# Cross attention of a two-layer perceiver: another order of VectorE's work in a head's step, and the wide running maximum folded by two maxima

## The reference, cut to what matters

```
q = (layernorm(x) @ Wq).reshape(256, 16 heads, 128) / sqrt(128)
k = (ctx @ Wk).reshape(4096, 16 heads, 128)
v = (ctx @ Wv).reshape(4096, 16 heads, 128)
scores = q @ k^T per head             # 16 x 256 x 4096
attn = softmax(scores, over the 4096)
x = x + (attn @ v).reshape(256, 2048) @ Wo
```

## Time and profile before

| | |
|---|---|
| median of 3 runs | 1687.32 us |
| profiled execution, its own time | 1687.09 us |
| its span | 1685.1 us |
| TensorE busy | 1607.2 us, 95% |
| VectorE busy | 1185.3 us, 70% |
| ScalarE busy | 720.1 us, 43% |
| GpSimd busy | 192.7 us, 11% |
| granted TensorE clock | 9 or more tenths of full speed in each of 40 slices, mean 0.997 |

### The profile page before, as it was taken

One profiled execution on the slowest core, in us unless ns is written; L12 is line 12 of the kernel. 1 busy time (PEld: TensorE's weight loads), 2 busy tenths in 40 slices (PEclk: granted clock), 3 DMA queues, 4 the chain that ended last, 5 costly groups with the idle time before them and its releaser, 6 DMA issues.

```text
span 1685.1 us, 23090 instructions
## 1 busy us (share of the span) xinstructions
PE 1607.2 (95%) x8798; PEld 1251.7 (74%) x8798; DVE 1185.3 (70%) x2124; ACT 720.1 (43%) x981; POOL 192.7 (11%) x247
## 2 busy tenths in 40 slices
PE   9999999999899999999999999989899999999998
PEld 8887878888787888877887888777766857555454
DVE  5546787888778788878878888989674682633333
ACT  4434454445444445444444545545441361322221
POOL 0001101011100101010010101111100054021110
PEclk9999999999999999999999999999999999999999
DMA  7876545454555545464444444333511335579994
GB/s 231 235 221 192 158 119 145 131 157 117 174 140 138 144 132 153 110 179 116 134 132 113 135 118 126 94 100 99 196 76 50 122 129 217 249 212 409 423 424 180
DMA packets 125660, 283.48 MB, mean 168 GB/s; under 512 B 7728, under 2 KB 83696, under 8 KB 119408
## 3 DMA queue, kind: packets, MB, share of 16 engines
q1 hardware_dynamic: 103248, 201.27, 35.8%
q0 software_dynamic: 22304, 80.75, 16.7%
HBM read 207.51 MB, written 74.48 MB: 167 GB/s over the span
## 4 chain that ended last, share of the span: by engine, by line
PE 44%; DVE 24%; issue 23%; ACT 5%; DMA 3%; POOL 2%; SPq 0%; DVEq 0%; POOLq 0%; ACTq 0%
PE bank L41 11%; PE bank L502 6%; PE bank L2320 5%; DVE esum L944 4%; DVE mx L879 4%; PE bank L470 4%; DVE e_parts L955 3%; DVE S L923 3%; ACT S L693 2%; DVE k_lo L863 2%; PE bank L526 2%; PE bank L2359 2%; PE bank L1886 2%; PE bank L2345 2%; DVE v_out L960 1%
## 5 line engine op out<-in xcount | busy, mean ns | idle before, releaser
L502 PE MATMUL bank<-wv_parts,cT_hi 128*128 128x512 f32 x1024 | 333.7, 389 | 0.4 <-DMA wv_parts<-wv_dram 0.4
L693 ACT ACTIVATE S<-S 128x1024 f32<-128x1024 f32 (+1 forms) x129 | 135.9, 1053 | 226.7 <-DVE S L923 226.5
L502 PEld LDWEIGHTS bank<-wv_parts,cT_hi 128*128 128x128 f32 x1024 | 192.3, 188 | 40.7 <-DMA wv_parts<-wv_dram 0.8
L944 DVE TENSOR_TENSOR esum<-esum,S 128x256 f32<-128x256 f32 x360 | 152.9, 425 | 77.1 <-ACT S L693 67.5
L470 PE MATMUL bank<-cT_hi,wk_hi 128*128 128x512 f32 x512 | 201.0, 392 | 0.2 <-DVE cT_lo L856 0.2
L470 PE MATMUL bank<-cT_lo,wk_hi 128*128 128x512 f32 x512 | 199.7, 390 | 0.0
L470 PE MATMUL bank<-cT_hi,wk_lo 128*128 128x512 f32 x512 | 199.5, 390 | 0.0
L502 PE MATMUL bank<-wv_parts,cT_lo 128*128 128x512 f32 x512 | 199.4, 389 | 0.0
L41 PE MATMUL bank<-q_hi,k_hi 128*128 128x256 f32 x512 | 149.2, 291 | 42.1 <-DVE k_lo L863 42.1
L879 DVE TENSOR_TENSOR mx<-mx,S 128x256 f32<-128x256 f32 x390 | 165.3, 424 | 24.2 <-ACT S L687 14.0
L702 ACT CAST e_parts<-S 128x1024 fp32r<-128x1024 f32 (+1 forms) x129 | 135.0, 1046 | 96.9 <-PE bank L526 89.7
(11 more groups left out here) (327 smaller groups left out, 2797.5 us busy)
## 6 DMA issues: line engine op xcount, KB each, us to landing
w<-in_w_moe SPq DMA_DIRECT2D x32, 2304.0 KB, 15.7
v_dram<-v_out SPq DMA_DIRECT2D x112, 512.0 KB, 4.8
v_back<-v_dram POOLq DMA_DIRECT2D x110, 512.0 KB, 4.2
ctx_nat<-in_ctx SPq DMA_DIRECT2D x8, 1024.0 KB, 5.4
ctx_raw<-in_ctxT SPq DMA_DIRECT2D x7, 1024.0 KB, 8.8
v_dram<-v_back SPq DMA_DIRECT2D x14, 512.0 KB, 4.8
v_late<-v_dram POOLq DMA_DIRECT2D x14, 512.0 KB, 3.7
wv_parts<-wv_dram POOLq DMA_DIRECT2D x6, 1024.0 KB, 8.3
```

The costliest lines, as they stand in the source:

```text
L502: t = e.matmul(banks[b][:], l, r, start=(c == 0 and m == 0), stop=(c == DT - 1 and m == 2))
L693: e.activation(Sj, Sj, ACT.Exp).then_inc(raised, 1)
L944: t = e.tensor_tensor(total, l, r, ALU.add)
```

## The change

VectorE's order in heads 0 to 11 is written anew. In a step from 2 on it becomes split_e, split_k and shift (in steps 2 and 6 shift first), keep_max, split_v, and then the sum of this same chunk; before, the sum of the next chunk stood ahead of split_v. In step 0 split_e stands ahead of split_v and sum_e, and ScalarE's order follows (raise and round of chunk 0 ahead of round_v). The reciprocal of `scale_o` becomes a function of its own, in step 2, and its product moves to step 3; the splits of Wo and of o move to step 4. In heads 12 to 14 split_k of chunk 0 moves ahead of fold_sum and of the first shift, and split_k of chunk 7 behind keep_max and split_e. GpSimd's `add_sums(h - 1)` stands in step 1 of head h for all heads, behind that step's load of values. The reduction of the wide maximum becomes two maxima, 128x512 and 128x256.

```diff
--- before.py
+++ after.py
@@ -749,11 +749,11 @@
                         if h:
                             store_scores(h, NCH - 1)
                         round_k(h + 1, 0)
-                        for u in units(h, 0):
-                            round_v(u)
                         if h:
                             raise_scores(h, 0)
                             round_e(h, 0)
+                        for u in units(h, 0):
+                            round_v(u)
                         raise_scores(h, 1)
                         continue
                     if j == 1:
@@ -897,16 +897,21 @@
                     own.wait(e)
                     own.done(e.tensor_tensor(mx_late[:], mx_late[:], Sj, ALU.max))
                 if j == NCH - 1:
-                    own.wait(e)
                     e.wait_ge(max_ready, h)
                     e.wait_ge(y_projected, h - 1)
-                    e.tensor_reduce(mx_folded[:], mx_late[:].rearrange("p a t -> p t a"), AX.X, ALU.max).then_inc(max_folded, 1)
+                    fold_max().then_inc(max_folded, 1)
+
+            def fold_max():
+
+                own.wait(e)
+                own.done(e.tensor_tensor(mx_late[:, 0:2], mx_late[:, 0:2], mx_late[:, 2:4], ALU.max))
+                own.wait(e)
+                return e.tensor_tensor(mx_folded[:], mx_late[:, 0], mx_late[:, 1], ALU.max)
 
             def keep_last_max():
 
-                own.wait(e)
                 e.wait_ge(max_ready, XH - 1)
-                own.done(e.tensor_reduce(mx_folded[:], mx_late[:].rearrange("p a t -> p t a"), AX.X, ALU.max))
+                own.done(fold_max())
                 own.wait(e)
                 e.wait_ge(scored, NH)
                 own.done(e.tensor_reduce(mx_late[:, 0, :], twin[:].rearrange("p (a t) -> p t a", t=T), AX.X, ALU.max))
@@ -972,9 +977,11 @@
                 to = esum_t if h == SUMMED else mx
                 e.tensor_tensor(to[:], esum_late[:, 0], esum_late[:, 1], ALU.add).then_inc(sum_folded, 1)
 
-            def scale_o(h):
+            def invert_row(h):
                 e.wait_ge(sum_ready, h + 1)
                 own.done(e.reciprocal(esum_t[:], esum_t[:]))
+
+            def scale_o(h):
                 own.wait(e)
                 e.wait_ge(o_moved, h + 1)
                 e.tensor_tensor(oT[:], oT[:], esum_t[:], ALU.mult).then_inc(scaled, 1)
@@ -1037,60 +1044,62 @@
                 if piece_at(j, 1) is not None:
                     split_piece(piece_at(j, 1))
             for h in range(LATE):
-                for j in range(NCH):
-                    if j == 0:
-                        split_q(h + 1)
-                        if h:
-                            keep_max(h, NCH - 1)
-                            move_o(h - 1)
-                        split_k(h + 1, 0)
-                        if h:
-                            shift(h, 0)
-                        for u in units(h, 0):
-                            split_v(u)
-                        shift(h, 1)
-                        sum_e(h, 0)
-                        if h:
-                            split_e(h, 0)
-                        continue
-                    if j == 1:
-                        sum_e(h, 1)
-                        split_k(h + 1, 1)
-                        shift(h, 2)
+                split_q(h + 1)
+                if h:
+                    keep_max(h, NCH - 1)
+                    move_o(h - 1)
+                split_k(h + 1, 0)
+                if h:
+                    shift(h, 0)
+                shift(h, 1)
+                if h:
+                    split_e(h, 0)
+                for u in units(h, 0):
+                    split_v(u)
+                sum_e(h, 0)
+                split_k(h + 1, 1)
+                shift(h, 2)
+                split_e(h, 1)
+                keep_max(h + 1, 0)
+                for u in units(h, 1):
+                    split_v(u)
+                sum_e(h, 1)
+                if half_at(h, 1) is not None:
+                    split_half(half_at(h, 1))
+                for j in range(2, NCH):
                     split_e(h, j)
-                    keep_max(h + 1, j - 1)
-                    if j > 1:
+                    if j == 4 and h:
+                        split_qo("wo", h - 1)
+                        split_o(h - 1)
+                    if j in (3, 4, 5):
                         split_k(h + 1, j)
+                        shift(h, j + 1)
+                    else:
                         if j + 1 < NCH:
                             shift(h, j + 1)
+                        split_k(h + 1, j)
                     if j == NCH - 1:
                         split_wk(h + 2)
-                    if j == 1:
-                        for u in units(h, j):
-                            split_v(u)
-                        sum_e(h, 2)
-                    else:
-                        if j + 1 < NCH:
-                            sum_e(h, j + 1)
-                        for u in units(h, j):
-                            split_v(u)
+                    keep_max(h + 1, j - 1)
+                    for u in units(h, j):
+                        split_v(u)
+                    if j == 3 and h:
+                        scale_o(h - 1)
+                    sum_e(h, j)
                     if half_at(h, j) is not None:
                         split_half(half_at(h, j))
                     if j == 2 and h:
-                        scale_o(h - 1)
-                    if j == 3 and h:
-                        split_qo("wo", h - 1)
-                        split_o(h - 1)
+                        invert_row(h - 1)
                     if j == NCH - 2:
                         split_qo("wq", h + 2)
             for h in range(LATE, XH - 1):
                 split_q(h + 1)
                 keep_max(h, NCH - 1)
                 move_o(h - 1)
+                split_k(h + 1, 0)
                 if h > LATE:
                     fold_sum(h - 1)
                 shift(h, 0)
-                split_k(h + 1, 0)
                 shift(h, 1)
                 split_e(h, 0)
                 sum_e(h, 0)
@@ -1103,14 +1112,15 @@
                         shift(h, j + 2)
                     if j + 1 < NCH:
                         sum_e(h, j + 1)
-                    if j in (1, NCH - 2):
+                    if j == 1:
                         split_k(h + 1, j + 1)
                     keep_max(h + 1, j - 1)
                     if j + 1 < NCH:
                         split_e(h, j + 1)
-                        if j not in (1, NCH - 2):
+                        if j > 1:
                             split_k(h + 1, j + 1)
                     if j == 2:
+                        invert_row(h - 1)
                         scale_o(h - 1)
                     if j == 3 and h == LATE:
                         split_qo("wo", h - 1)
@@ -1217,9 +1227,7 @@
                         load_v(n + 3)
                     if h and j == 0 and n != TAIL:
                         largest_score(h)
-                    if j == NCH - 1 and h < LATE:
-                        add_sums(h)
-                    if j == 0 and LATE < h < XH - 1:
+                    if j == 1 and 0 < h < XH - 1:
                         add_sums(h - 1)
 
         CROSS_DONE = TT * 3
```

## The result

The changed kernel takes 1700.49 us, the median of 4 runs (1698.52 to 1700.57), against 1687.51 us for the kernel before (4 runs, 1687.03 to 1690.25): a ratio of 1.0071, 95% interval 1.0053 to 1.0088. The profiled execution took 1698.52 us. Forecast were 1684.0 us and a range of 1672 to 1693.

A forecast was written before the change was run, and what follows sets the result against it. TensorE was taken as the bound, with VectorE's order setting its stalls. From 1687.09 us, 12.6 won in early heads and 9.3 lost in heads 12 to 14 gave 1683.8, plus 0.2 for the median: 1684.0 us, range 1672 to 1693.

The forecast's parts named there:

- What bounds the kernel: Whole kernel: TensorE is the bound and VectorE's order sets its stalls, 48 us for ten early heads.
- the steady step: Early heads, new order: k_lo comes 1.2 us early, so S(3), S(4), S(7) wait no more.
- The wait that comes: Step 1 of each head: VectorE stands still 4.4 us for GpSimd's sum, S(1) is late; 3.0 us lost a head.
- Heads 4 and 8: No V in step 0: S(2) 4.6 us late, W(h,1) 0.2, S(0) keeps 1.6, W(h,0) 0.4; 6.8 each.
- Heads 12 to 14: VectorE has nearly no slack, so losses come out at S(4): 4.9, 2.6 and 1.8 us, 9.3 lost together.
- The fold: Late heads: the wide maximum's reduction takes 1.1 us for 2.01; the last fold, on the path, saves 0.8.
- The shift beside GpSimd's sum: Late heads: the shift took 2.12 us beside GpSimd's sum, against 1.21; in the new order it stands alone.
- the bound of 1640: Lower bound if the wait for the sum costs nothing: -3.0 x 9, and some 11 in the late heads.
- (a): Early heads' step 2: VectorE loses 0.9 at the first shift and S(2) stalls too; 1692 us, slower, chance 0.24.
- (d): Early heads' waits stay, as ScalarE's k_hi was their cause; only the losses count, 1723 us; chance 0.03.
- (b): Heads 12 to 14 find slack again and lose only what S(1) shows, 4.7 us; 1679 us; chance 0.17.
- (c): The wait for the sum hardly binds; all but S(0)'s waits go, 1640 to 1665 us; chance 0.08.

The follow-up runs named there:

- the filled kernel: The changed kernel plus identity matmuls on TensorE, 11 ahead of S(1) in heads 1 to 11, 16 ahead of S(2) in heads 4 and 8: 1686.21 us.
- the seventh experiment: The changed kernel with add_sums in step 0, plus 9 identity matmuls ahead of W(h,0) in heads 12 to 14: 1641.78 us, against 1639.94 without them.
- the eighth experiment: The changed kernel with add_sums in step 0, plus one reduction of the wide maximum in place of the two maxima: 1645.73 us, against 1639.94.

## Why the prediction was wrong, point by point

- **What bounds the kernel, and the steady step:** right. The waits at S(3), S(4), S(7) and W(h,0) of the early heads are gone, apart from the 0.2 at W(4,0) and W(8,0) (forecast 0.4).
- **The wait that comes:** right in place, chain and price. VectorE stands still 4.49 us for 4.4, the sum takes 1.75 for 1.74, the gap at S(1) is 2.6. A head where the clock stays up takes 72.41 us, W(6,0) to W(7,0), for 72.3.
- **Heads 4 and 8:** right in place; the gap at S(2) is 5.4 where 4.6 were given.
- **The term that failed is the price of that wait:** "With 0.1 for a restart the new loss is 3.0 us in each head". It was taken as idle time alone. The prediction traded 44 waits of at most 1.7 us for 14 of up to 5.4 with nearly the same sum, and left out that TensorE comes back from the long ones at half clock. In the ten heads that is 11.2 us: 734.7 to 745.9 between the filled kernel and the changed one. With it the ten heads come to -10.4 + 11.2 = +0.8; the rest of the measured +3.9, 3.1 us, is S(2)'s 0.8 in two heads, 0.1 of the period in the other eight, and some 0.7 that isn't accounted for. The span missed the forecast by 14.7 us: these 11.2 and 3.1, and 0.4 ahead of W(1,0). The clock turned the sign of the ten heads: with the wait kept and the clock held up they are 7.2 us faster than before.
- **Heads 12 to 14:** 9.3 us lost, forecast 9.3, and in part that is luck. Head 12 goes as forecast: k_lo(4) comes 25.9 us behind W(12,0) for 21.6, which with the late W(12,0) is the 5.4 of the prediction. But up to the columns' sums of head 14 the heads have lost 10.8 us (1.0 by the late W(12,0), then 161.7 us for 151.9), and 1.4 came back behind them: there TensorE is at half clock in both kernels, for 6.8 us before and for 3.4 us after, and needs 6.6 and 5.2 us to W(15,0). One link was missed, S(2) waits 1.8 us for ScalarE's store; VectorE sets the pace to S(4) all the same. That the half clock in the heads themselves (mean 0.96 up to the columns' sums) cost nothing is argued from the seventh experiment, which tested it at W(h,0) only.
- **The fold:** it takes 1.1 us for 2.0, as forecast, but by the eighth experiment it is worth 1.6 us in the three heads and not 2.7.
- **The shift beside GpSimd's sum:** in the changed kernel no shift takes over 1.22 us, so it does stand alone, as the prediction said; with the sum in step 0 it takes 2.12 again in heads 13 and 14.
- **Two slips in the working**, which change little above: the bound of 1640 comes to 1646 by its own terms (1684 - 27 - 11), and head 13 to 2.8 and not 2.6 (3.3 less a wait of 0.5).
- **Rivals:** none named the clock. (a) put its loss at S(2) of the early heads; S(2) of heads 1 to 3 waits for nothing. (d), also on the slower side, kept the early waits, and they went. (b) had heads 12 to 14 lose only half of what they lost, and (c) came true only when the sum was moved.
- **The range** reached 1693 by rival (a) and ended 7.5 us short. Its bounds were all for idle time. The kernel before had two signs to ask with. It fills waits elsewhere with matmuls that compute nothing (`stay_awake`, six of them ahead of W(15,0)). And its trace has a row: the clock fell to 0.5 at 1181.5, in its one wait of 3.9 us (the columns' sums wait for esum_t), as this row of a stretch of the kernel before shows:

```profile
1181.54:1188.37 6.83, 6.37 (x18) 4.34 (x19) 6.30 (x10) 5.69 (x8) 0.92 (x2) 0.50 0.37 117
```

The granted clock fell behind 2.6 us of waiting in five heads of nine, in another execution with the same waits in six of nine, and behind 4.5 us in nine of nine. What tells those heads from the others is not shown here. The Trainium skill (TensorE: Matmul & The Clock Gate, Terms) puts the penalty at about the time in the throttled state times the share of pulses left out. An estimate by that rule, with the half that the rows at 0.50 show, is 15.4 us for the 30.7 us of the ten heads. The runs have 11.2 there, and nothing for the stretches at the start of heads 12 to 14, where TensorE waits for VectorE anyway; so here the rule gives an upper bound. Of the missing 4 us a good half can be seen. In heads 4 and 8 the first 1.2 and 0.7 us of the stretch lie in the wait before S(2), which takes 0.9 from the estimate. And behind S(1) at full clock W(h,1) has a wait that at half clock is gone: from S(1) to W(2,1) it is 1.74 us, for 1.43 in a step without a wait, which takes 0.3 in each of five heads. The rest isn't placed.

## What to carry to other kernels

Before an instruction is moved onto an in-order queue, read what the one ahead of it waits for: a 1.75 us sum behind a load that waits for a matmul cost 60 us over 14 heads, and either of two places ahead of that load gives them back. Where TensorE is the bound, waits are not to be added up alone: here few long ones cost more than many short ones of nearly the same sum, so look at the granted clock behind the longest waits of the trace and price a new long wait with it. Where another engine is the bound, as in heads 12 to 14, half clock at the start of the head cost nothing, and filling TensorE's wait brought nothing.

## What wasn't expected of the hardware

TensorE fell to half clock for 3.4 us even behind waits of 2.0 to 2.25 us (W(12,0) to W(14,0) of the kernel with the sum in step 0), while the waits of up to 1.8 us in heads 0 to 14 of the kernel before never brought it down. The length of one wait doesn't settle it: the clock also fell behind waits of 1.8 us at S(2) of head 12 and S(2) of head 14 of the changed kernel (at 1048.6 and 1161.3 us), behind one of 1.65 us in the eighth experiment (1175.3), and in the kernel before, in the last block, at 1509.2, where the longest wait close ahead is 1.1 us. Eleven short matmuls that compute nothing (22 in the trace), 2.6 us long, kept the clock at 1.00 in nine heads, sixteen did so in heads 4 and 8, and together they made the changed kernel 14 us faster than with the waits left empty.
